# Second cross attention of a Perceiver layer stack: one mask product in eight moves from GpSimd to VectorE

## The reference

```python
# second cross attention: B=1, t=256 queries, T=4096 keys, 16 heads of 16
content = jnp.einsum('bthd,bThd->bhtT', q + r_w_bias, k)
rel = _relative_shift(jnp.einsum('bthd,bThd->bhtT', q + r_r_bias, pe))
attn = (content + rel) * (1.0 / math.sqrt(HEAD_DIM))
attn = attn * mask - 10000000000.0 * (1.0 - mask)
p = jax.nn.softmax(attn, axis=-1)
out = jnp.einsum('bhtT,bThd->bthd', p, v).reshape(b, t, DMODEL)

# linear attention of the first layer, its end
res = out + x                       # x: the normed tokens
return (res - mu) / jnp.sqrt(var + 1e-12) * gamma + beta   # added to the tokens
```

## Time and profile before

| what | value |
|---|---|
| runs of before, us | 1364.95, 1361.10, 1364.61; median 1364.61 |
| the profiled execution, us | 1368.14 |
| its span from the first to the last instruction, us | 1366.3 |
| mean granted TensorE clock of the span | 0.931 |
| PE busy | 1127.7 us, 83% |
| ACT busy | 893.6 us, 65% |
| DVE busy | 822.7 us, 60% |
| POOL busy | 632.3 us, 46% |
| the first and last masked product (L1950) begin at | 734.4 and 1190.2 us |

### The profile page before, as it was taken

One profiled execution on the slowest core, in us unless ns is written; L12 is line 12 of the kernel. 1 busy time (PEld: TensorE's weight loads), 2 busy tenths in 40 slices (PEclk: granted clock), 3 DMA queues, 4 the chain that ended last, 5 costly groups with the idle time before them and its releaser, 6 DMA issues. The chain is left out here.

```text
span 1366.3 us, 25496 instructions
## 1 busy us (share of the span) xinstructions
PE 1127.7 (83%) x8423; PEld 690.0 (50%) x8423; DVE 822.7 (60%) x1502; ACT 893.6 (65%) x1204; POOL 632.3 (46%) x297
## 2 busy tenths in 40 slices
PE   7677877859999859989977888888888888857798
PEld 3344443433444346678852444544455444434687
DVE  5688888870111166462235787888878888835312
ACT  3599999978999624433323788888888888524110
POOL 2277887850000005000004899999999999800000
PEclk9899999979999878989985899999999999878899
DMA  7875555538654070024458999999899999433140
GB/s 244 246 231 130 132 122 130 131 98 165 119 99 89 13 254 8 1 78 153 154 218 283 309 308 323 325 333 325 311 319 334 328 322 317 152 114 127 47 139 8
DMA packets 97052, 257.53 MB, mean 188 GB/s; under 512 B 11193, under 2 KB 41306, under 8 KB 85467
## 3 DMA queue, kind: packets, MB, share of 16 engines
q1 hardware_dynamic: 96992, 256.79, 60.3%
HBM read 165.31 MB, written 91.92 MB: 188 GB/s over the span
## 5 line engine op out<-in xcount | busy, mean ns | idle before, releaser
L1950 POOL TENSOR_TENSOR xb_row<-xb_row,w_mask 128x1024 f32<-128x1024 f32 x128 | 419.2, 3287 | 240.0 <-DVE xb_row L1980 238.7
L1980 DVE TENSOR_TENSOR xb_row<-xb_cont_ps,xb_row 128x1024 f32<-128x1024 f32 x128 | 156.7, 1224 | 83.2 <-PE xb_cont_ps L1773 73.3
L1773 PE MATMUL xb_rel_ps<-xb_kk,xb_qq 32*128 32x512 f32 x496 | 148.9, 678 | 35.0 <-ACT xb_out L1898 33.3
L561 DVE TENSOR_REDUCE xa_stats<-xa_b_ps 128x1 f32<-128x1024 f32 x128 | 155.8, 1219 | 27.2 <-PE xa_b_ps L477 25.8
L1991 DVE CUSTOM_DVE_ANT_0 xb_row<-xb_row,xb_minus 128x1024 f32<-128x1024 f32 x128 | 170.9, 1335 | 0.0
L1903 ACT ACTIVATE xb_row<-xb_row,xb_ntop 128x2048 f32<-128x2048 f32 x64 | 128.3, 2005 | 51.1 <-DVE xb_ntop L1997 51.1
L1773 PE MATMUL xb_cont_ps<-xb_kk,xb_qq 32*128 32x512 f32 x528 | 160.2, 684 | 1.5 <-DVE xb_qq L2052 1.1
L880 ACT ACTIVATE xa_probs<-xa_psT,xa_t_now 128x1024 f32<-128x1024 f32 x128 | 141.2, 1114 | 18.4 <-PE xa_psT L837 18.3
L1898 ACT COPY xb_out<-xb_rel_ps 128x1024 f32<-128x1024 f32 x124 | 124.7, 1005 | 39.8 <-PE xb_rel_ps L1773 26.8
L1909 ACT COPY xb_turned<-xb_turn_ps 128x1024 f32<-128x1024 f32 x126 | 127.5, 1012 | 26.9 <-PE xb_turn_ps L1817 24.8
L529 ACT ACTIVATE xa_exps<-xa_b_ps,xa_stats 128x1024 f32<-128x1024 f32 x128 | 140.7, 1102 | 6.6 <-DVE xa_stats L561 6.6
(11 more groups left out here) (367 smaller groups left out, 1823.9 us busy)
## 6 DMA issues: line engine op xcount, KB each, us to landing
xb_row<-rel_scores SPq DMA_DIRECT2D x128, 512.0 KB, 6.3
rel_scores<-xb_out SPq DMA_DIRECT2D x32, 1024.5 KB, 5.6
rel_scores<-xb_out SPq DMA_DIRECT2D x32, 1024.0 KB, 5.6
b_e_w<-in_L_ffn_e_w SPq DMA_DIRECT2D x32, 513.0 KB, 3.4
w_w<-in_L_ffn_w SPq DMA_DIRECT2D x24, 512.0 KB, 4.9
xa_k<-first_parts SPq DMA_DIRECT2D x24, 384.0 KB, 5.1
value_rows<-xa_values SPq DMA_DIRECT2D x16, 544.0 KB, 6.1
xb_kk<-key_blocks SPq DMA_DIRECT2D x17, 512.0 KB, 7.8
```

The source lines that it names most:

```text
L561: nc.vector.tensor_reduce(stats[:, c % 2, 0, u:u + 1], ps[:, slot % 4], AX, ALU.min).then_inc(s["min_ready"], 1)
L1773: mm = nc.tensor.matmul(out[:, k * BANK:(k + 1) * BANK], qq[rows, b, kind, t * P:(t + 1) * P], kk[rows, b, half], start=True, stop=True)
L1950: nc.gpsimd.tensor_tensor(row[:, held(c), at:at + SUB], row[:, held(c), at:at + SUB], mask[:, t, half * HALF + at:half * HALF + at + SUB], ...
L1980: nc.vector.tensor_tensor(row[:, held(c), at:at + SUB], cont_ps[:], row[:, held(c), at:at + SUB], ALU.add).then_inc(s["cont_out"], 1)
```

## The change

1. In units with u = 3, part 1 (one part in eight), VectorE adds `row` onto `cont_ps` with the result in PSUM, waits for that (`added_here`), and multiplies `cont_ps` by the mask into `row`; only then is `cont_out` counted. GpSimd skips this part and counts `masked` twice at part 0. `top_of` of that part waits for `cont_out` as well.
2. The last slots: `at_end` holds for the last three units in place of two, so that part 1 of unit 61 is turned into `rel_ps` as well; ScalarE copies it from there, and VectorE those of the last two units (`by_vector`), as before. In slots 64 to 67 (`ending`) TensorE turns both parts of unit n-3 at the start of the slot, ahead of its wait for the sums of unit n-4.
3. The second half of `minus` is made in slot -4 in place of slot -1.
4. In the linear attention the addition of beta to the tokens stands ahead of the wait for the keys, not behind the bias of the values.

```diff
--- before.py
+++ after.py
@@ -1052,13 +1052,13 @@
             step(nc.vector.tensor_scalar(red[:], red[:], PI_BELOW, -PI_BELOW, ALU.min, ALU.max))
             dve.sem_inc(s["angles"], 1)
             dve.wait_ge(s["loaded"], 80)
+            step(nc.vector.tensor_tensor(f.x[:], f.x[:], gain[:, 1].unsqueeze(1).to_broadcast([P, NT, D]), ALU.add))
             dve.wait_ge(s["k_gelu"], 1)
             rotate(step, kr, k)
             dve.sem_inc(s["krot_ready"], 1)
             dve.wait_ge(s["v_mm"], 1)
             step(nc.vector.tensor_tensor(v[:], tiles(3), bv[:].unsqueeze(1).to_broadcast([P, NT, D]), ALU.add))
             dve.sem_inc(s["v_sb"], 1)
-            step(nc.vector.tensor_tensor(f.x[:], f.x[:], gain[:, 1].unsqueeze(1).to_broadcast([P, NT, D]), ALU.add))
             dve.wait_ge(s["q_gelu"], 1)
             rotate(step, qr, q)
             dve.sem_inc(s["qrot_ready"], 1)
@@ -1625,7 +1625,7 @@
             names = ("small_loaded", "var_ready", "root_ready", "dve_steps", "xn_ready", "xnT_mm", "xnT_sb",
                      "w_turned", "q_mm", "q_made", "minus_set", "fill_out",
                      "rel_mm", "rel_out", "cont_mm", "cont_out", "masked", "halves_max", "top_ready",
-                     "exp_done", "turned", "weighed", "sums_sb", "gathered", "sums_read", "zero_set", "top_begun", "top_kept", "row_free")
+                     "exp_done", "turned", "weighed", "sums_sb", "gathered", "sums_read", "zero_set", "top_begun", "top_kept", "row_free", "added_here")
             s = {n: f.sem("b_" + n) for n in names}
             k_loaded, v_loaded = ([f.sem(f"{n}_loaded{b}") for b in range(2)] for n in ("k", "v"))
             turned_sb = [f.sem(f"b_turned_sb{n}") for n in range(2)]
@@ -1683,7 +1683,15 @@
 
             def at_end(n):
 
+                return isinstance(n, int) and n >= UNITS - 3
+
+            def by_vector(n):
+
                 return isinstance(n, int) and n >= UNITS - 2
+
+            def masked_here(u, part):
+
+                return u == U - 1 and part == 1
 
             def makes_queries(n, c):
 
@@ -1840,6 +1848,7 @@
                                      ).then_inc(s["gathered"], 1)
 
                 def slot(p, c, n):
+                    ending = isinstance(n, int) and n >= UNITS
                     if runs(n, U - 1) and (n is None or n > 0):
                         relative(p, c + U - 1, 1)
                     if c % U == 0 and (n is None or n < UNITS):
@@ -1849,6 +1858,9 @@
                         pe.wait_ge(k_loaded[(c // U + 1) % 2], 16 * (p + (c // U + 1) // 2 + 1))
                     if runs(n, 0):
                         content(p, c, 0)
+                    if ending and runs(n, -BEHIND):
+                        turn(p, c - BEHIND, 0)
+                        turn(p, c - BEHIND, 1)
                     if runs(n, -BEHIND - 1):
                         pe.wait_ge(s["sums_sb"], where(p, c - BEHIND - 1)[0] + 2)
                     if n is None or n >= 0:
@@ -1856,7 +1868,7 @@
                             make_queries(2 * p + c // U + 2, c // U % 2)
                     if runs(n, -BEHIND - 1):
                         bring_together(p, c - BEHIND - 1)
-                    if runs(n, -BEHIND):
+                    if runs(n, -BEHIND) and not ending:
                         turn(p, c - BEHIND, 0)
                     if runs(n, U):
                         relative(p, c + U, 0)
@@ -1867,7 +1879,8 @@
                     if runs(n, 0):
                         content(p, c, 1)
                     if runs(n, -BEHIND):
-                        turn(p, c - BEHIND, 1)
+                        if not ending:
+                            turn(p, c - BEHIND, 1)
                         weigh(p, c - BEHIND, 0)
                         weigh(p, c - BEHIND, 1)
 
@@ -1906,14 +1919,15 @@
                     n, head, u, b, t, half = where(p, c)
                     act.wait_ge(s["turned"], 2 * (n + ROWS_HELD) + part + 1)
                     act.wait_ge(s["weighed"], 2 * n + part + 1)
-                    nc.scalar.copy(turned[:, part].rearrange("p k n -> p (k n)"), turn_ps[:]).then_inc(turned_sb[part], 1)
+                    src = rel_ps if at_end(n) and part == 1 else turn_ps
+                    nc.scalar.copy(turned[:, part].rearrange("p k n -> p (k n)"), src[:]).then_inc(turned_sb[part], 1)
 
                 def slot(p, c, n):
                     if runs(n, -BEHIND):
                         copy_turned(p, c - BEHIND, 0)
                     if runs(n, U):
                         evacuate(p, c + U, 0)
-                    if runs(n, -BEHIND) and not at_end(where(p, c - BEHIND)[0]):
+                    if runs(n, -BEHIND) and not by_vector(where(p, c - BEHIND)[0]):
                         copy_turned(p, c - BEHIND, 1)
                     if runs(n, -1):
                         exponentials(p, c - 1)
@@ -1945,11 +1959,14 @@
                         return
                     n, head, u, b, t, half = where(p, c)
                     for part in range(2):
+                        if masked_here(u, part):
+                            continue
                         at = part * SUB
+                        halves_done = 2 if masked_here(u, part + 1) else 1
                         pool.wait_ge(s["cont_out"], 2 * n + part + 2)
                         nc.gpsimd.tensor_tensor(row[:, held(c), at:at + SUB], row[:, held(c), at:at + SUB],
                                                 mask[:, t, half * HALF + at:half * HALF + at + SUB],
-                                                ALU.mult).then_inc(s["masked"], 1)
+                                                ALU.mult).then_inc(s["masked"], halves_done)
 
                 slots(pool, slot)
 
@@ -1977,6 +1994,14 @@
                     dve.wait_ge(rel_back[u][part], 16 * (head + 1))
                     dve.wait_ge(s["cont_mm"], 2 * n + part + 1)
                     at = part * SUB
+                    if masked_here(u, part):
+                        nc.vector.tensor_tensor(cont_ps[:], cont_ps[:], row[:, held(c), at:at + SUB], ALU.add
+                                                ).then_inc(s["added_here"], 1)
+                        dve.wait_ge(s["added_here"], head + 1)
+                        nc.vector.tensor_tensor(row[:, held(c), at:at + SUB], cont_ps[:],
+                                                mask[:, t, half * HALF + at:half * HALF + at + SUB],
+                                                ALU.mult).then_inc(s["cont_out"], 1)
+                        return
                     nc.vector.tensor_tensor(row[:, held(c), at:at + SUB], cont_ps[:], row[:, held(c), at:at + SUB],
                                             ALU.add).then_inc(s["cont_out"], 1)
 
@@ -1984,6 +2009,8 @@
 
                     n, head, u, b, t, half = where(p, c)
                     dve.wait_ge(s["masked"], 2 * n + part + 1)
+                    if masked_here(u, part):
+                        dve.wait_ge(s["cont_out"], 2 * n + part + 2)
                     if part == 0 and isinstance(n, int) and n == 0:
                         dve.wait_ge(s["minus_set"], NT)
                     dve.sem_inc(s["top_begun"], 1)
@@ -2013,10 +2040,10 @@
                 def slot(p, c, n):
                     if n is not None and n < 0:
                         evacuate_right(c + U)
+                        if n == -U:
+                            set_minus(1)
                         if makes_queries(n, c):
                             make_queries(1, 1)
-                        if n == -1:
-                            set_minus(1)
                     if runs(n, -BEHIND - 1):
                         sums_out(p, c - BEHIND - 1)
                     if runs(n, 0):
@@ -2032,7 +2059,7 @@
                     if n is None or n >= 0:
                         if makes_queries(n, c):
                             make_queries(2 * p + c // U + 2, c // U % 2)
-                    if runs(n, -BEHIND) and at_end(where(p, c - BEHIND)[0]):
+                    if runs(n, -BEHIND) and by_vector(where(p, c - BEHIND)[0]):
                         copy_last_turned(p, c - BEHIND)
 
                 def copy_last_turned(p, c):
```

## The result

The changed kernel takes 1380.43 us (median of 1384.56, 1383.30, 1377.37 and 1377.56), against 1364.34 for the kernel before in the same session. The ratio is 1.0117, with a 95% interval of [1.0097, 1.0136]: 16.1 us slower, 13.2 to 18.6. The forecast was 1378.7, with 1374 to 1383 as its own range.

What follows compares the result with a forecast made beforehand. A chain of waits through VectorE, ScalarE, TensorE and two GpSimd products, not GpSimd's busy time, sets the 28.43 us head. 17.5 - 2.7 - 0.7 = +14.1 us on 1364.6 gives 1378.7, own range 1374 to 1383.

Steps and rivals of the forecast that it cites:

- The second pass: VectorE's added product in slot 3 lies on the chain: +1.25 us a head, 14 heads, +17.5 us.
- GpSimd's product at 0: Taking GpSimd's product away in slot 3 is worth 0 in the repeating part, bounds 0 to 1.4 us a head.
- Rivals 1 and 2: 1: GpSimd paces the loop, middle 1355, chance 0.15; 2: maxima's waits absorb the delay, 1370.2 or 1365, chance 0.13.
- the prediction's chain: Links between exponentials of 14.26, 7.32 and 6.84 us make a head; two part 0 products on it hold maxima.
- Rival 3: TensorE's granted clock falls, with longer idle ahead of slot 0: 18 us more for such a head, 1397; chance 0.06.
- 84 and 80% are close: Argument against a clock fall: TensorE's busy share would only go from 84% to 80%.
- The end: Last slots of the cross attention: last exponential 1.4 us earlier, two rounds 1.3 less; together -2.7, bounds -1.4 and -4.
- drowned delay of head 14: In head 14 the second pass's 1.25 us was to cost nothing, hidden by a read-back wait.
- the forecast's path through the read-back: Head 14's next addition waits 1.74 us for its read-back DMA, issued ahead of slot 3, so the delay drowns.
- The two rounds behind it: Behind the last exponential, each round loses the 0.66 us from the weighing to the next transpose: -1.3 us.
- the 9.8 to the end of the keeping: Last exponential to the end of the keeping should take about 9.8 us, not 11.1.
- Beta's addition: In the linear attention, 0.69 us on VectorE goes into a 1.54 us wait for the keys: -0.7, or 0.

Runs made afterwards that it cites:

- e9: The kernel before, unchanged, run once more for a second profile: 1363.91 us.
- e10: The changed kernel with four idle 128x128 matmuls added on TensorE behind the transposes of each slot 0: 1375.90 us, ratio 1.0098.
- e6: The changed kernel with the second pass at unit 0, part 1 in place of unit 3, part 1: 1368.74 us, ratio 1.0033.
- e7: The changed kernel with the second pass at unit 3, part 0 in place of part 1: 1365.21 us, ratio 1.0004.
- e1: The changed kernel without the second pass, GpSimd making all eight products and the other edits kept: 1360.00 us, ratio 0.9953.
- e3: The changed kernel with GpSimd skipping its product in one part of eight and nobody making it: 1360.82 us, ratio 0.9961.
- e4: The changed kernel with GpSimd making all eight products while VectorE makes its one too: 1382.18 us, ratio 1.0112.
- e11: The changed kernel once more, unedited, on the same chip as the run with four idle matmuls: 1378.27 us, ratio 1.0118.

## Why the prediction was right, and where it was off

**The second pass, forecast at 1.25 a head: confirmed.** Measured 1.27 in a head of full clock, by the gap, the pass and the maximum nearly as they were written down (0.04, 1.23, 1.14; the 1.25 of the forecast is 1.23 + 0.03, rounded down). The addition into PSUM is as long as the one into SBUF. From the first exponential to unit 58's, e9 to e10 (both at full clock in all 14 heads between exponentials of unit 2) is 415.19 to 432.56 = +17.4. By the forecast it is 15 passes, one of which is to drown later, +18.8. What is missing is that e9 has three longer heads of its own (28.82, 28.85 and 29.00), the last two with waits for read-backs, which e10 doesn't have. That the place decides is shown by e6 and e7: the three kernels give VectorE the same two passes, and share the other edits, which by themselves gain 6.4 us (e1). Against the kernel before they stand at +16.1, +4.5 and +0.5 us. Against e1, by the ratios, the pass so costs some 22, 11 and 7 us, and from the first exponential to unit 58's 27.6 (with the falls of the clock; 18.4 in e10), 10.3 and 5.8.

**GpSimd's product at 0: confirmed** by e3 and e4. Rivals 1 and 2 are out with them and with the timeline: no head got shorter, and the two maxima that are held begin later together with the products that hold them. The hold weighs less than the prediction's chain says: in the head before the one of the earlier trace rows the maximum of slot 1 is not held (1.22 us at 889.83), and the link is 14.29 us all the same.

**TensorE's clock: the term that was mis-sized.** Rival 3 named the place, a longer idle stretch in slot 0, but priced it as all or nothing, up to 18 us a head with a chance of 0.06. It did happen, in part: the fall lasts 3 to 4 us each time and costs 1.2 to 1.5 us a head, in 7 of 14 heads of the first profiled run and 3 of the second. For the first that is some 9 us (441.76 less e10's 432.56). On the medians e11 stands 2.4 us over e10 (1378.27 and 1375.90, six runs each, whose ranges overlap), some two heads. The two runs at 1377.4 and the two at 1384 in the first session would fit two and seven such heads, though only one of the four has a profile. "84 and 80% are close" was the wrong argument: 81% was measured, and the clock fell. The profile before had shown such a fall, in its own last head, and I didn't ask the one-microsecond stretches for it. The Trainium skill's TensorE: Matmul & The Clock Gate, section A second HAM failure mode: psum-queue depth-cycling, tells of a kernel whose frequent short idle stretches between groups of matmuls made the clock go up and down. The heads here agree, and e11 against e10 shows what it costs. What decides in which head the clock falls is open.

**The end, forecast at -2.7 with the drowned delay of head 14 besides, was too large.** Against the first profiled run it is -4.3, near what it should be (-2.7 - 1.25 = -3.95), but that agreement is an accident: much of it is the fall of the clock in before's last head. Against e9 it is 43.04 to 42.21 (e10), -0.8, and this is how it comes about. The delay of head 14 did not drown. The wait for the DMA, 1.74 in the earlier trace rows and 1.08 in e9, is gone in e10, and unit 59's exponential comes 6.38 us behind unit 58's in place of 7.36. But unit 60's comes 13.89 behind in place of 13.98, so the delay is back one unit later, and the forecast's path through the read-back was not the one that paced the exponentials there. The last exponential comes 1.15 us earlier (31.15 behind unit 58's for 32.30), near the 1.4 that was written down. The two rounds behind it, forecast at -1.3, are where the edit loses to another fall of the clock. At full clock, in e6 and e7, it takes from the last exponential to the beginning of the last keeping 8.9 us where e9 has 10.7, -1.8. In the changed kernel, with the fall at 1216, it is 11.3, and in e10, with one at 1205, 11.1. So the 9.8 to the end of the keeping that I gave is not what was seen. What makes TensorE's clock fall there in some of these kernels and not in others is open.

**Beta's addition at -0.7: consistent.** VectorE's wait for the keys shrank and nothing came in its place:

```profile
482.83 0.43 DVE L1024 SCALAR_TENSOR_TENSOR la_kr<-la_k,la_rope 128x256 f32<-128x256 f32 x1 [0.56 <-ACT la_k L1012]
```

0.56 for the 1.54 of the earlier trace rows. From the start of the linear attention to the first exponential the kernels without the edit take 271.7 to 271.9, those with it 269.4 to 271.1. That is more than 0.7 in most, and what the rest is wasn't tried. `minus` was not tried by itself.

**What the forecast could not hold.** Behind the last keeping the span goes on for 157.9 us before and 155.1 after, with no edit there. e1, with the same edit of the last slots, has 158.2, so it isn't that edit alone. It seems to go with the clock: one of the next stage's stretches at half clock lasts from 1239 to 1249 before, and its counterpart from 1257 to 1264 after. The cause is open. Without these -2.8 and the -2.1 ahead of the linear attention, the changed kernel's first profiled run would stand 21 us above before's, and the forecast would have been exceeded by more. So +14.1 for a measured +16.1 is in part luck. In the two profiled runs the repeating part gave +26.8 for the forecast's 18.8, the difference being the clock, and the parts with no edit gave -4.9 against it. The experiments say the same by the medians: the other edits gain 6.4 us and not 3.4 (e1), and the second pass costs some 22 with its falls of the clock, not 17.5.

## What to carry to other kernels

Before moving work from an idle-looking engine to another, write the chain of one period down by start times, and price the two places apart: here the same pair of instructions cost some 22, 11 or 7 us by the part at which they stood, and a product less on the engine with the most busy time was worth nothing. A chain that waits for VectorE makes TensorE idle as well; where its granted clock is 1.00 with a busy share in the eighties, look at single microseconds behind its longest waits, in the profile before too, and count a few falls of 1.3 us into the range. A few idle matmuls in the wait kept the clock up here. Four, which ended at about the end of the wait (940.28 and 940.21), were worth about 2.4 us on the medians; eight ran past it and brought nothing.

## What was new of the hardware

- The granted clock fell to 1.2 GHz for 3 to 4 us in a loop that keeps TensorE 81% busy (24.06 of 29.70 us) with no wait of its matmuls above 1.3 us, in 21 of 56 periods with the same waits. With the head of 28.43 us and TensorE 84% busy it fell in none of 28 (the kernel before, two profiles), though waits of 1.0 to 1.3 us occur there too.
- With four idle 128x128 matmuls in a wait of 0.8 to 1.3 us it stayed at 1.00 in all 14 heads of that run.
- VectorE writes 128x1024 fp32 into PSUM, from PSUM and SBUF, in 1.23 us, and the pass is as long beside a product of GpSimd, while the maximum with two SBUF inputs takes turns with that product (1.34 and 1.68 for 1.22).
